# Low parts of the tokens on GpSimd, and another order of SyncE's transfers, in the expert part of a whitening, attention and mixture-of-experts kernel

## The reference

```python
x = _L0_conv_ref(x, gamma, beta)        # mean and covariance over all tokens, whitening in groups of 16 channels
t = _to_tokens(x)
t = t + _L1_attn_ref(_ln_t(t), ...)     # attention in a window of 33 tokens, then a layer norm
t = t + _L1_ffn_ref(_ln_t(t), ...)      # mixture of experts, on the normed tokens:
# probs = softmax(tokens @ router_w.T);  combine = the two largest, normed, else 0
# out = tokens
# for e in range(8):
#     h = gelu(tokens @ w1[e] + b1[e]);  y = h @ w2[e] + b2[e]
#     out = out + combine[:, e:e + 1] * y
```

## Time and profile before

| | |
|---|---|
| median of 3 runs | 1103.78 us (1103.2 to 1103.79) |
| the profiled execution | 1107.27 us |
| its span, first to last instruction | 1105.5 us |
| mean granted TensorE clock over the span | 0.952 |
| TensorE, VectorE, ScalarE, GpSimd busy | 94%, 83%, 50%, 13% of the span |

### The profile page before, as it was taken

One profiled execution on the slowest core, in us unless ns is written; L12 is line 12 of the kernel. 1 busy time (PEld: TensorE's weight loads), 2 busy tenths in 40 slices (PEclk: granted clock), 3 DMA queues, 4 the chain that ended last, 5 costly groups with the idle time before them and its releaser, 6 DMA issues. The chain is left out here.

```text
span 1105.5 us, 25729 instructions
## 1 busy us (share of the span) xinstructions
PE 1036.0 (94%) x9158; PEld 713.7 (65%) x9158; DVE 912.7 (83%) x2575; ACT 551.0 (50%) x917; POOL 148.3 (13%) x179
## 2 busy tenths in 40 slices
PE   7948999999999999999699999999999999999997
PEld 7926777777777777777555555555555555555554
DVE  6943888888888788887789899899889989988885
ACT  0014555565665456553355555555555555555553
POOL 7021233232232222232100000000000000000000
PEclk9966999999999799996599999999999999999999
DMA  9603555555555446544112222222222222222221
GB/s 284 247 9 84 135 133 141 141 125 143 134 141 143 119 118 151 138 120 119 51 42 71 72 70 73 67 71 72 75 67 69 74 68 75 68 70 73 75 72 47
DMA packets 244773, 111.89 MB, mean 101 GB/s; under 512 B 199392, under 2 KB 242656, under 8 KB 243888
## 3 DMA queue, kind: packets, MB, share of 16 engines
q1 hardware_dynamic: 235456, 96.91, 35.4%
q10 hardware_dynamic: 8064, 12.85, 3.4%
q0 software_dynamic: 1136, 0.56, 0.2%
HBM read 71.60 MB, written 38.67 MB: 100 GB/s over the span
## 5 line engine op out<-in xcount | busy, mean ns | idle before, releaser
L587 ACT ACTIVATE arena<-p,b_s 128x896 f32<-128x896 f32 x224 | 212.4, 996 | 15.3 <-PE p L1115 13.0
L891 DVE TENSOR_TENSOR arena<-arena,p 128x896 f32<-128x896 f32 x150 | 162.4, 1083 | 27.7 <-ACT arena L587 17.1
L1115 PE MATMUL p<-thl,w_hi 128*128 128x448 f32 x448 | 146.9, 409 | 0.4 <-DVE thl L863 0.4
L1140 PE MATMUL p<-arena,w_s 128*64 128x448 f32 x600 | 133.7, 545 | 0.3 <-DVE arena L891 0.3
L1125 PE MATMUL p<-arena,selector 128*128 128x448 bf16 x448 | 124.8, 360 | 6.5 <-DVE arena L891 2.9
L1115 PE MATMUL p<-thl,w_lo 128*128 128x448 f32 x448 | 128.0, 367 | 0.0
L600 ACT ACTIVATE thl<-arena 64x896 fp32r<-64x896 f32 x56 | 53.3, 952 | 103.8 <-DMA arena<-tn_spill 103.8
L1115 PEld LDWEIGHTS p<-thl,w_hi 128*128 128x128 f32 x448 | 85.5, 191 | 14.3 <-issue 0.8
L480 POOL TENSOR_TENSOR yb<-yb,bet 128x448 f32<-128x448 f32 x56 | 59.2, 1057 | 259.0 <-DVE xn_s L829 259.0
L594 ACT ACTIVATE arena<-arena 64x448 bf16<-64x448 bf16 x56 | 32.3, 576 | 118.7 <-DVE arena L859 118.6
L891 DVE TENSOR_TENSOR sq<-arena,p 128x896 f32<-128x896 f32 x74 | 80.1, 1082 | 13.6 <-ACT arena L587 9.6
(11 more groups left out here) (180 smaller groups left out, 1813.9 us busy)
## 6 DMA issues: line engine op xcount, KB each, us to landing
tn_spill<-tnt_s ACTq DMA_DIRECT2D x56, 224.0 KB, 2.7
arena<-tn_spill SPq DMA_DIRECT2D x56, 224.0 KB, 3.4
t_s<-tn_spill SPq DMA_DIRECT2D x56, 224.0 KB, 2.5
arena<-in_x_dram SPq DMA_DIRECT2D x112, 96.0 KB, 2.6
xn_rows<-xn_s SPq DMA_DIRECT2D x56, 192.0 KB, 2.1
out_dram<-arena SPq DMA_DIRECT2D x112, 96.0 KB, 1.8
resid<-in_x_dram SPq DMA_DIRECT2D x6, 1568.0 KB, 14.4
v_a<-xn_rows SPq DMA_DIRECT2D x56, 168.0 KB, 3.4
```

What stands on the lines that cost most here:

```text
L587: a.activation(hid[:, j % 2, :].rearrange("p (h n) -> p h n", h=H), (p34 if j % 2 == 0 else p56)[:, :, 0:CH], ACT.Gelu, bias=b1_s[:, j:j + ...
L891: v.tensor_tensor(gated[u % 3].rearrange("p (h n) -> p h n", h=H), hid[:, j % 2, :].rearrange("p (h n) -> p h n", h=H), p01[:, :, 0:CH], A ...
L1115: last = t.matmul(bank[:, h, 0:CH], w[:, 128 * j:128 * (j + 1)], thl[:, c, h, :], start=(k == 0), stop=(k == 1))
L1140: last = t.matmul(p2[64 * h:64 * h + 64, 0:CH], w2_s[:, j, :], gated[u % 3][:, h * CH:(h + 1) * CH], start=False, stop=(j == 3))
```

## The change

`low` leaves VectorE's program. GpSimd gets a loop of its own behind its two memsets at the end of the second stage, which does the same subtraction for each of the 56 groups, as soon as `high` of the group is done. VectorE's calls of `low` (before the first step, and in each step between `route` and `finish`) are taken out.

On SyncE, the loop is written out straight for all groups, and the tokens of group g + 1 are issued ahead of the rows of g and the results of g - 2. They still wait for `high` and `low` of the group that used the buffer before.

```diff
-            def step3(g, c, has):
-                if has(0):
-                    wait(sp, s_hi, g - 1)
-                    wait(sp, s_lo, g - 1)
-                    sp.dma_start(tn_in[:, c, :].rearrange("p (h n) -> p h n", h=H),
-                                 spill[g].rearrange("(h p) n -> p h n", h=H)).then_inc(s_ti[c], 16)
-                    if not isinstance(g, int):
-                        rows(g, c)
-                if has(2):
-                    wait(sp, s_fin, g - 1)
-                    for tile, tokens in pieces(out_tokens, g - 2, fin[:, c, :]):
-                        sp.dma_start(tokens, tile).then_inc(s_out[c], 16)
+            def tokens_in3(g):
+                wait(sp, s_hi, g - 1)
+                wait(sp, s_lo, g - 1)
+                sp.dma_start(tn_in[:, g % 2, :].rearrange("p (h n) -> p h n", h=H),
+                             spill[g].rearrange("(h p) n -> p h n", h=H)).then_inc(s_ti[g % 2], 16)
+
+            def results(g):
+                sp.wait_ge(s_fin, g + 1)
+                for tile, tokens in pieces(out_tokens, g, fin[:, g % 2, :]):
+                    sp.dma_start(tokens, tile).then_inc(s_out[g % 2], 16)
...
-            for c in range(2):
-                rows(c, c)
-            with sp.Fori(1, G // 2) as i:
-                for c in range(2):
-                    step3(i * 2 + c, c, lambda d: True)
-            for c in range(2):
-                step3(G + c, c, lambda d: d > 0)
+            for g in range(2):
+                rows(g, g)
+            tokens_in3(2)
+            for g in range(2, G):
+                if g + 1 < G:
+                    tokens_in3(g + 1)
+                rows(g, g % 2)
+                results(g - 2)
+            for g in range(G - 2, G):
+                results(g)
...
             walk(pool, step, 7, G, 4, after)
 
+            pool.wait_ge(s_zero, 3)
+            pool.wait_ge(s_t2, G)
+            for g in range(G):
+                c = g % 2
+                pool.wait_ge(s_hi, g + 1)
+                v.tensor_tensor(thl[64:128, c], tn_in[:, c].rearrange("p (h n) -> p h n", h=H),
+                                thl[0:64, c].bitcast(f32), ALU.subtract).then_inc(s_lo, 1)
...
-            def low(g, c):
-                wait(dve, s_hi, g + 1)
-                v.tensor_tensor(thl[64:128, c], tn_in[:, c].rearrange("p (h n) -> p h n", h=H),
-                                thl[0:64, c].bitcast(f32), ALU.subtract).then_inc(s_lo, 1)
-
...
-                    if more:
-                        low(g + 1, 1 - c)
...
-                    low(0, 0)
```

More of the change, by code:

```diff
@@ L374, in rows @@
                 sp.dma_start(tn_rows[:, c, :], spill[g]).then_inc(s_tr[c], 16)
-            def step3(g, c, has):
-                if has(0):
-                    wait(sp, s_hi, g - 1)
-                    wait(sp, s_lo, g - 1)
-                    sp.dma_start(tn_in[:, c, :].rearrange("p (h n) -> p h n", h=H),
-                                 spill[g].rearrange("(h p) n -> p h n", h=H)).then_inc(s_ti[c], 16)
-                    if not isinstance(g, int):
-                        rows(g, c)
-                if has(2):
-                    wait(sp, s_fin, g - 1)
-                    for tile, tokens in pieces(out_tokens, g - 2, fin[:, c, :]):
-                        sp.dma_start(tokens, tile).then_inc(s_out[c], 16)
-            for c in range(2):
-                sp.wait_ge(s_sp[c], 16)
-                step3(c, c, lambda d: d == 0)
+            def tokens_in3(g):
[8 more added lines that the diff above has]
+            for g in range(2):
+                sp.wait_ge(s_sp[g], 16)
+                tokens_in3(g)
             for k in range(3):
```

## The result

The changed kernel took 1176.78 us (median of 4 runs, 1169.91 to 1188.01) against 1103.78 before: slower, ratio 1.0618, 95% interval 1.056 to 1.0677. Measured again later it took 1166.38 against 1104.37, ratio 1.0557 (1.0503 to 1.061). The first ratio leaves out the execution of 1188.01 as a slow one and takes in a fourth run of the kernel before (1113.40), so it is not the quotient of the two medians. The forecast was 1157.

A forecast was written before the change was run, and what follows sets the result against it. TensorE's own work was taken to set about 9.63 us a group, the rest adding 9 us in sum. Terms -7.4 + 58.8 + 1.9 = +53.3 gave 1160.6 profiled, forecast 1157; range 1145 to 1182, with rival A 1095 to 1182.

The forecast's parts named there:

- the gain: Expert part: low leaving VectorE brings periods to 9.63 except two steps where the tanh wait stays; 7.4 us saved.
- SyncE's order is worth nothing alone: Expert part: early tokens end ScalarE's 1.96 us wait a group, but bring nothing on the path by themselves.
- The place of the meeting: Each usual expert step: GpSimd's low starts at t+2.82, 0.19 us before the second splitting subtraction, which waits; 49 steps.
- A: Rival, splitting in expert steps: the second subtraction gets in before GpSimd's low, only the gain is left; 1096 to 1098, chance 0.24.
- B: Rival, expert steps: a held step lets the next go free, so half the steps are held; +23 us, 1127, chance 0.08.
- C: Rival, whole expert part: VectorE's time was hidden and GpSimd's is too, nothing counts; 1102 to 1106, chance 0.04.
- a tie: Two expert steps where ScalarE's late gelu leaves open whether low or the subtraction starts first; not counted among the 49.
- the order repeats in each step: Expert part: both engines hang on TensorE's products of the same step, so low meets the splitting alike in each.
- The size of a hold: Expert steps: low lasts 1.97 us, the subtraction ends 1.57 later, the third spread 1.20 later; 49 steps, 58.8 us.
- the tanh ahead of the doubling: Two expert steps where the routing's tanh stands before the doubling of the routing weights: 0.84 us each, 1.7 in all.
- no clock would be below full: Profile of the changed kernel: no TensorE clock below full, since the gaps are 1 us; otherwise time above the range.
- The start: Start of the expert part: low of group 0 holds a VectorE instruction and TensorE with it; +1.9 us, bounds 0 and 2.5.

The follow-up runs named there:

- the cure: The changed kernel, but GpSimd's low of group g+1 also waits for gate 1 of g: 1097.47 us, ratio 0.9938 to the kernel before.
- the one-input kernel: The changed kernel with the second splitting subtraction replaced by a cast of its first input (third routing-weight part wrong): 1097.39 us, ratio 0.994.
- the repeat: The changed kernel, unaltered, measured again on the chip of the later runs: 1166.38 us, ratio 1.0557 to the kernel before.

## Why the prediction was right, and where its sum fell short

*What bounds the kernel, and the gain.* TensorE sets 9.63, and VectorE adds 7 to 9 us in all. The gain was put at 7.4; the cure shows 7.1 (538.82 - 531.74). That SyncE's order is worth nothing alone was right too. That a run can tell 0.2% from no change was not: with 10 or 12 runs of a kernel the intervals are 0.3 to 0.5% either way.

*The place of the meeting.* Low was to start at t+2.82 and did at t+2.81; every one of the 49 steps counted had a hold, so rivals A (the subtraction first) and B (some steps only) fell. C fell with them. The six periods without a hold were foreseen: the five with the routing's tanh and the last. In the two of them that I had called a tie, the order of rival A did come about, by 0.01 us (timeline of the changed kernel):

```profile
747.46 0.23 DVE L886 TENSOR_TENSOR arena<-arena 128x63 f32<-128x63 f32 x1
747.47 2.19 POOL L507 TENSOR_TENSOR thl<-arena,thl 64x896 fp32r<-64x896 f32 x1 [10.28 <-ACT thl L609]
```

The subtraction keeps its 0.23 us and low is the longer one. So A was right on what would happen, and wrong on who comes first in the other steps. In one of the 49, early in the expert part, low met the first splitting subtraction instead of the second:

```profile
590.89 2.10 POOL L507 TENSOR_TENSOR thl<-arena,thl 64x896 fp32r<-64x896 f32 x1 [8.92 <-ACT thl L609]
590.93 2.14 DVE L882 TENSOR_TENSOR arena<-comb,arena 128x63 f32<-128x63 f32 x1
```

Gate 0 of this step (t = 588.08) came 0.35 us later behind its gelu than usual, and the splitting with it. The hold ends at the same place (t+4.99), but three instructions of the splitting still follow instead of one, and the step is 0.5 us longer than the other held ones: 11.54 in the one-input kernel, 11.55 in the repeat. I had said that the order repeats in each step.

*The size of a hold.* This term was mis-sized. I took 1.97 us for GpSimd's subtraction from 193 and 448 columns; it lasts 2.08 to 2.12. And I let VectorE follow 0.02 behind GpSimd, as in the earlier trace rows; it follows 0.08 to 0.09 behind. The subtraction ends at t+4.99, not t+4.81, and the third spread starts at t+6.83, not t+6.64. A step costs 1.39 to 1.40, not 1.20: 49 x 0.2 = 10 us, about as much as the repeat's medians (+62.0) lie above the forecast's +53.3. The first measurement's +73 has some 10 us more from outside the expert part, of which the forecast says nothing. The expert part adds up: 55 x 9.63 + 49 x 1.40 + 2 x 0.79 + 2.2 = 602.0. The 0.79 is the tanh ahead of the doubling, forecast as 0.84. The 2.2 was not in the sum: 0.5 of it is the step just shown, the rest TensorE's clock.

*The clock.* Right behind that step comes a stretch of 3 us at half clock (windows of the changed kernel: length, busy us by engine, clock):

```profile
590.00:596.00 6.00, 4.38 (x25) 2.35 (x21) 5.86 (x10) 2.36 (x3) 2.10 (x1) 0.97 0.10 20
596.00:599.00 3.00, 3.00 (x11) 1.11 (x12) 1.36 (x2) 0.46 (x1) 0.00 (x0) 0.50 0.45 116
```

TensorE idled for some 1.6 us of the 6 before it, 1.44 of them in one piece ahead of `back`. I had written that no clock would be below full; for this stretch that was wrong. The two periods there are 11.74 and 12.46 (11.55 and 12.73 in the repeat, which has the same meeting and the same stretch). No other profile has a clock below 0.9 in its expert part in any microsecond. But the one-input kernel has the same step (TensorE idle for 1.45 us ahead of `back`, and for 1.6 us of 6) at full clock throughout. There no hold stands in the step before it, while in the changed kernel one does. So that gap alone did not lower the clock; whether it takes the holds before it was not tried.

*The start.* The hold I put at +1.9 happened, and little of it is seen at the first b2 product (timeline of the changed kernel):

```profile
558.31 0.62 DVE L853 TENSOR_TENSOR tn_s<-resid,sm 128x448 f32<-128x448 f32 x1
...
558.48 2.38 POOL L507 TENSOR_TENSOR thl<-arena,thl 64x896 fp32r<-64x896 f32 x1 [2.10 <-ACT thl L609]
...
558.84 2.04 DVE L855 TENSOR_TENSOR comb<-yb,sm 128x7 f32<-128x7 f32 x1
```

L855 stands 1.9 us too long; low itself takes 0.28 more than usual, since it starts while L853, with two SBUF inputs, is running. The first layer starts 1.34 later behind the last normed tokens than before (4.47 against 3.13). But the first b2 product comes 15.04 after them (15.37 in the repeat), hardly later than before (15.03): before, TensorE stayed at half clock (0.50) up to about 555.8, that is through the whole start; here the same stretch had 0.84 and 0.66 in its later two thirds. In the repeat and in the cure, which have this hold too, the clock also rose early (0.80 and 0.66; 0.75 and 0.66), and with the first low back on VectorE it stayed at half (0.54 in the last third). So the faster clock took back most of the delay here. Why it rises earlier was not shown, and it doesn't hang on the hold alone: with SyncE's order alone, without the hold, it rose early as well, and the first b2 product came after 14.17 us. What the hold is worth under the same clock these profiles can't tell.

## What to carry to other kernels

Before work goes to GpSimd, list what VectorE does in the very microseconds in which GpSimd will read: an instruction with two SBUF inputs that comes second stands there until GpSimd's instruction is done, however short it is itself. If it comes first, GpSimd waits instead, and that costs nothing where GpSimd has time. What counts is the instant, not the load: the same 2.1 us cost 1.4 a step at one place and nothing 2.4 us later, and one added wait moved it. Two edits that are harmless alone can meet, here an earlier transfer and a moved subtraction; time such parts singly before the sum.

## What the runs showed of the hardware

VectorE and GpSimd exclude each other by instruction: 63 elements that take 0.225 us lasted 1.98 us (median) beside a GpSimd subtraction that had started first, with GpSimd's own length unchanged (2.08 to 2.12). The other way round, GpSimd's subtraction took 2.28 beside a 392-element VectorE instruction begun 0.23 us earlier, which kept its 0.56. With two GpSimd instructions back to back VectorE got in between them. A memset on GpSimd did not hold the subtraction up. A held instruction of 392 elements ended 0.42 us behind GpSimd, one of 63 elements 0.08 to 0.09, one of 7 elements 0.02 to 0.03. Single-input instructions of VectorE differ: casts of 63 float32 to bfloat16 ran beside GpSimd (0.23 us), a tensor_scalar of 49 float32 did not (0.99 instead of 0.18, ending 0.05 behind GpSimd). The Trainium skill (SBUF — State Buffer, Who interferes with whom) describes both the two-input case and single-source instructions in a two-port mode, and these runs agree with it; which of the single-source ones meet its conditions was not tried further.

Undisturbed, a tensor_tensor on GpSimd took 2.08 to 2.12 us for 64 partitions of 896 columns, reading partitions 0 to 63 and writing 64 to 127 as float32r, and 1.15 for 448 of them, where 128 partitions of 448 float32 took 1.06. SyncE's straight code issues four result transfers in 2.09 us, the loop in 2.41 (medians); in the changed kernel no engine waited for a transfer between 600 and 1100 us.
